# Sixteen-head attention as one stream of quads, with the second pass two quads behind the first

## The chip, the cores and the metric

The program runs on one core of a Trainium2 chip. The metric is the device time in microseconds (us); lower is better. TensorE is called PE, VectorE DVE, ScalarE ACT, GpSimd POOL, and SP is the engine that issues the DMAs.

## The reference

Eight layers are added to a residual stream `x` of 8 sequences of 512 tokens of 128 features in float32. The change is in two of them, both 16-head softmax attention with heads of 8 features:

```python
x = x + _L0_attn_a_ref(_layernorm(x), ...)   # causal: where(tril, q@k.T, -inf) / sqrt(128)
x = x + _L0_ffn_ref(_layernorm(x), ...)
x = x + _L0_attn_b_ref(_layernorm(x), ...)   # not causal, rope on the input, q@k.T / sqrt(8)
x = x + ...                                  # six more layers, untouched
# in both: q,k,v = xn@W.T + b per head; softmax(q@k.T) @ v; all heads @ Wo.T + bo
```

## The kernel before

An *item* is a sequence (8), a *quad* is four heads (4 in an item, 32 in a layer). `attention` is built twice: `aa` (causal) and `ab` (with rope).

- Preparation of an item: layer norm (DVE L450 to L471, POOL L236, L252), transposition to `xT` (PE L345, ACT L315), projections q and k (PE L353, ACT L319) and v (PE L359, DVE L480, POOL L248). q and k are each cut into three bfloat16 parts by four dependent instructions (`split_part`, L214): q on POOL, k on DVE. SP stores the six parts in DRAM (`store`, L279) and loads them back, rearranged, as `QS` and `KS` in two halves of eight heads, 18 DMAs of 64 KB each (`stack`, L286).
- First pass (`first_scores` L362): scores with queries on the partitions, two banks of PSUM; DVE takes the row maxima straight from them (L488). Of a quad that is 16 matmuls of 512 keys in `ab`; in `aa` 128 to 512 keys, and each is followed by a mask matmul (L377). When a quad is done DVE makes its negated maxima in two bfloat16 parts (`nm`, L492, L494), PE transposes them (L384), DVE copies them out (L500), SP stores them in DRAM and, when that has landed, loads them into two rows of `QS` (`send_nm`, L297). They all go through SP's one queue, in which `stack` and `store` stand too.
- Second pass (`scores` L387): scores with keys on the partitions, maxima subtracted by those two rows; it needs `nm_loaded` of its quad. In `aa` a mask matmul follows each (L402). ACT takes the exponentials (L332, four buffers `probs`), and PE multiplies them with V (`sum_keys` L406), one group of 4 heads per key tile, each head in its own 32 columns of the array. DVE copies the sums out (L506), PE turns them (`tail`), DVE divides (L511, L513). After four quads come `oT` and `y` (L434) and the residual (L520).

The order is one list `STEP` that all engines walk, each in order and each waiting on semaphores. Preparation, first pass, second pass and output are four stages, each one whole item behind the other: a quad's second pass comes four quads after its first. Eleven steps run in all, the middle four as a hardware loop.

Of the kernel before, what the change touches and what calls it, by code (L numbers as in the profile page):

```python
# [25 lines left out]
P = 128  # L26
# [56 lines left out]
SHIFT_ROWS = 2  # L83


def score_units(causal):

    if not causal:
        first = [(qt, (j,), 512, 512) for qt in range(4) for j in range(4)]
        second = [(kt, pair, 512, 512) for kt in range(4) for pair in ((0, 1), (2, 3))]  # L90
        return first, second
# [4 lines left out]
    return first, second  # L96


def attention(core, items, w, causal, rope, scale):
    nc, X, ps = core["nc"], core["X"], core["ps"]  # L100
    first, second = score_units(causal)
    N1, N2 = len(first), len(second)
# [32 lines left out]

# [18 lines left out]
    nm_ready, nmT_ready = sem("nm_ready"), sem("nmT_ready")  # L154
    nm_loaded = [sem(f"nm_loaded{i}") for i in range(QUADS)]
    scores_ready, scores_free = sem("scores_ready"), sem("scores_free")
    probs_free, sums_free = sem("probs_free"), sem("sums_free")
    STACK_DMAS = 2 * SPLITS * SPLITS

    PREP, PASS1, PASS2, OUT = range(4)  # L160

    extra = {(0, 0): [("ln1", 0), ("vaug", 0)], (0, N2 // 2): [("ln2", 0)], (1, 0): [("xT", 0)],
             (1, 3): [("q", 0)], (1, 5): [("k", 0)], (2, 0): [("k split", 0)], (2, 1): [("k split", 1)],
             (2, 2): [("k split", 2)], (2, 3): [("k split", 3), ("store", 0), ("half0", 0)],
             (3, 3): [("v", 0)]}

    last_quad = {(0, 1): [("last sums", 3), ("last nm", 3)], (0, 2): [("last tail", 3)],  # L170
                 (0, 3): [("oT", 0)], (0, 5): [("y", 0)]}
    STEP, waiting = [(0, "half1", 1)], []
    for hq in range(QUADS):
        for i in range(N2):
            mine = range((i * N1 + N2 - 1) // N2, ((i + 1) * N1 + N2 - 1) // N2)
            STEP += [(hq, "first", u) for u in mine[:1]]
            STEP += [(hq, "scores", i)]
            STEP += [(hq, "first", u) for u in mine[1:]]
            STEP += waiting
            waiting = []  # L180
            if i == N2 - 1 or second[i + 1][0] != second[i][0]:
                waiting.append((hq, "sum", second[i][0]))
            if hq and i == 1:
                STEP += [(hq, "sums", hq - 1), (hq, "nm", hq - 1)]
            if hq and i == 2:
                STEP += [(hq, "tail", hq - 1)]
            STEP += [(hq, what, j) for what, j in last_quad.get((hq, i), [])]
            STEP += [(hq, what, j) for what, j in extra.get((hq, i), [])]
    STEP += waiting

    stage_of = {"ln1": PREP, "ln2": PREP, "xT": PREP, "q": PREP, "k": PREP, "k split": PREP, "v": PREP,
                "store": PREP, "half0": PREP, "half1": PASS1,
                "vaug": PASS1, "first": PASS1, "nm": PASS1,
                "scores": PASS2, "sum": PASS2, "sums": PASS2, "tail": PASS2,
                "last nm": PASS2, "last sums": OUT, "last tail": OUT, "oT": OUT, "y": OUT}
    USES = ("xT", "q", "k", "v", "nm", "last nm", "tail", "last tail", "oT", "y")

    def walk(eng, does):


        def step(s, par, on):
            m = (4 * done(s, PREP, items) + 3 * done(s, PASS1, items) + 4 * done(s, PASS2, items)
                 + 3 * done(s, OUT, items))
            for hq, what, i in STEP:
                k = stage_of[what]
                if on(k):
                    part = does.get(what.replace("last ", ""))
                    if part is not None:
                        part(s - k, hq, i, (par - k) % 2, m)
                    if what in USES:  # L210
                        m = m + 1
        run_steps(eng, items, 4, step, before=1)

    def split_part(eng, a, n, m, i):  # L214


        src, parts = proj[a], split[a]
        if i == 0:


            eng.wait_ge(misc_free, m + 1)
            wait(eng, stack_loaded[1], 16 * STACK_DMAS * n)
            eng.tensor_tensor(parts[0][:], src[:], core["zeros"][:], ALU.add)
        if i == 1:
# [9 lines left out]
    def gpsimd(g):
# [6 lines left out]
        def vaug(n, hq, i, par, m):  # L241


            if isinstance(n, int) and n == 0:
                g.wait_ge(set_up, 1)
# [1498 lines left out]
```

## Time and profile before

| | |
|---|---|
| median of 3 runs | 2516.82 us (2515.82 to 2524.92) |
| profiled execution, first to last instruction | 2520.3 us |
| PE / DVE / ACT / POOL busy | 1994.8 / 1683.3 / 850.6 / 502.1 us |
| layer `aa`, first score to residual | 61.3 to 568.2 us |
| layer `ab`, first score to residual | 671.0 to 1239.8 us |

The profiled execution's own time is its span, 2520.3 us; nothing outside the span is shown for it. Busy shares are averages over nine layers with different limits, so the two attention layers are read by themselves.

### The profile page before, as it was taken

What the parts mean: (1) busy time and instruction counts of PE and PEld (TensorE: products, weight loads), DVE (VectorE), ACT (ScalarE), POOL (GpSimd) and SP (SyncE); (2) the same over time, 40 slices, a digit from 0 to 9 for tenths busy, and PEclk for the clock granted to TensorE, in tenths of its full rate; (3) what the DMA queues carried; (4) which work ended last, traced back from release to release, by engine and by line L of the source; (5) the groups of instructions that cost most, each with busy time, mean ns of one, the idle gap of its engine ahead of it and who ended that gap; (6) DMA issues with size and microseconds to landing.
All of it is one profiled execution on the core that took longest, in us unless ns stands there. A gap on an engine that the chain in (4) does not pass through costs nothing. (4 is left out here: it accounts for less than half of the span.)

```text
span 2520.3 us, 37035 instructions
## 1 busy us (share of the span) xinstructions
PE 1994.8 (79%) x12009; PEld 1174.1 (47%) x12009; DVE 1683.3 (67%) x3783; ACT 850.6 (34%) x1324; POOL 502.1 (20%) x421
## 2 busy tenths in 40 slices
PE   1688887885388998899669999999999856668566
PEld 0244444443122222222237777777778534445344
DVE  1666666646388877887257776677666469945897
ACT  0033343353025545556542222322232322223122
POOL 1111111003221111110120000000000446620566
PEclk9788888896569989999789999999999978879787
DMA  6333333200323222221000000000000000000000
GB/s 151 61 54 56 53 53 52 52 2 2 50 52 52 52 52 52 43 46 15 1 0 1 1 1 1 1 1 2 1 1 1 1 0 1 0 1 0 5 13 17
DMA packets 71728, 63.01 MB, mean 25 GB/s; under 512 B 11528, under 2 KB 69384, under 8 KB 71560
## 3 DMA queue, kind: packets, MB, share of 16 engines
q1 hardware_dynamic: 71560, 60.87, 13.7%
q8 instruction: 93, 1.52, 0.3%
q14 instruction: 75, 0.61, 0.1%
HBM read 45.51 MB, written 15.20 MB: 24 GB/s over the span
## 5 line engine op out<-in xcount | busy, mean ns | idle before, releaser
L488 DVE TENSOR_REDUCE ab_M<-ps 128x1 f32<-128x512 f32 x512 | 331.3, 686 | 91.8 <-PE ps L372 76.4
L332 ACT ACTIVATE ab_probs<-ps 128x1024 f32<-128x1024 f32 x256 | 260.3, 1024 | 250.9 <-PE ps L399 248.9
L488 DVE TENSOR_REDUCE aa_M<-ps 128x1 f32<-128x384 f32 (+3 forms) x352 | 216.3, 639 | 157.6 <-PE ps L377 144.9
L372 PE MATMUL ps<-ab_KS,ab_QS 72*128 72x512 bf16 x512 | 217.4, 430 | 74.6 <-DVE ab_M L488 40.0
L332 ACT ACTIVATE aa_probs<-ps 128x1024 f32<-128x1024 f32 (+1 forms) x192 | 168.4, 882 | 284.3 <-PE ps L402 282.2
L372 PE MATMUL ps<-aa_KS,aa_QS 72*128 72x384 bf16 (+3 forms) x512 | 156.1, 340 | 121.3 <-DMA aa_KS<-aa_parts_dram 89.5
L1439 PE MATMUL ps<-gate_up,fp_xT 128*128 128x352 f32 x256 | 127.9, 665 | 91.3 <-DVE fp_xh L1481 90.3
L372 PEld LDWEIGHTS ps<-ab_KS,ab_QS 72*128 72x128 bf16 x512 | 51.3, 100 | 263.1 <-DVE ab_M L488 205.3
L416 PE MATMUL ps<-ab_probs,ab_V 128*9 128x512 f32 x1024 | 145.6, 643 | 21.3 <-ACT ab_probs L332 15.9
L399 PE MATMUL ps<-ab_QS,ab_KS 74*128 74x512 bf16 x512 | 160.1, 399 | 0.5 <-ACT ab_probs L332 0.5
L372 PEld LDWEIGHTS ps<-aa_KS,aa_QS 72*128 72x128 bf16 x512 | 54.5, 107 | 192.2 <-DMA aa_KS<-aa_parts_dram 65.3
L1007 PE MATMUL ps<-la_V,la_S 128*128 128x65 f32 x1024 | 142.5, 262 | 0.1
L1007 PEld LDWEIGHTS ps<-la_V,la_S 128*128 128x128 f32 x1024 | 134.6, 191 | 0.5 <-issue 0.5
L1439 PEld LDWEIGHTS ps<-gate_up,fp_xT 128*128 128x128 f32 x256 | 68.0, 278 | 137.8 <-issue 69.6
L399 PE MATMUL ps<-aa_QS,aa_KS 74*128 74x256 bf16 (+3 forms) x512 | 130.7, 320 | 0.8 <-ACT aa_probs L332 0.4
L984 PEld LDWEIGHTS ps<-la_phiq,la_phik 64*128 64x128 f32 x1024 | 108.6, 187 | 45.7 <-issue 22.5
L1071 DVE TENSOR_TENSOR la_S<-ps,keep_kq 128x512 f32<-128x512 f32 x128 | 84.8, 686 | 64.9 <-PE ps L984 64.9
L984 PE MATMUL ps<-la_phiq,la_phik 64*128 64x128 f32 x1024 | 126.2, 285 | 0.0
L937 ACT ACTIVATE la_attnT<-ps 128x512 f32<-128x512 f32 x64 | 38.2, 597 | 256.0 <-PE ps L1015 256.0
L558 POOL TENSOR_TENSOR la_rstd<-la_vare,mhalf 128x4 f32<-128x4 f32 x16 | 16.1, 1008 | 518.0 <-DVE la_vare L553 518.0
L377 PE MATMUL ps<-mask_qk,ident 128*128 128x128 bf16 x512 | 112.8, 244 | 0.0
L416 PE MATMUL ps<-aa_probs,aa_V 128*9 128x512 f32 (+3 forms) x1024 | 98.8, 459 | 6.1 <-DVE aa_C L506 2.4
(286 smaller groups left out, 3981.3 us busy)
## 6 DMA issues: line engine op xcount, KB each, us to landing
aa_QS<-aa_parts_dram SPq DMA_DIRECT2D x144, 64.0 KB
aa_KS<-aa_parts_dram SPq DMA_DIRECT2D x144, 64.0 KB
ab_QS<-ab_parts_dram SPq DMA_DIRECT2D x144, 64.0 KB
ab_KS<-ab_parts_dram SPq DMA_DIRECT2D x144, 64.0 KB
aa_parts_dram<-aa_splitq SPq DMA_DIRECT2D x24, 128.0 KB, 1.8
aa_parts_dram<-aa_splitk SPq DMA_DIRECT2D x24, 128.0 KB, 1.8
ab_parts_dram<-ab_splitq SPq DMA_DIRECT2D x24, 128.0 KB, 1.8
ab_parts_dram<-ab_splitk SPq DMA_DIRECT2D x24, 128.0 KB, 1.8
```

Of the source, the lines that this page charges most:

```text
L332: act.activation(v(probs[r][:]), v(src), ACT.Exp, scale=scale).then_inc(scores_free, 1)
L372: last = pe.matmul(ps[:, FIRST + b, o * stride:o * stride + width], QS[par][0:ROWS, h, qt * P:(qt + 1) * P], KS[par][0:ROWS, h, 0:width], ...
L377: last = pe.matmul(ps[:, FIRST + b, c:c + P], core["ident16"][:], core["mask_qk"][:], start=False, stop=True)
L399: last = pe.matmul(ps[:, bank, c:c + width], KS[par][0:rows, h, kt * P:(kt + 1) * P], QS[par][0:rows, h, 512 - width:512], start=True, sto ...
L416: last = pe.matmul(ps[32 * j:32 * j + DH + 1, SUMS, 512 - width:512], V[par][:, kt, 4 * hq + j, :], probs[(N2 * hq + i) % 4][:, o * stride ...
L488: v.tensor_reduce(M[:, heads[0]:heads[-1] + 1, qt], src, AX.X, ALU.max).then_inc(max_free, 1)
L558: g.tensor_tensor(rstd[par][:], vare[par][:], mhalf[:, 0:per], ALU.pow).then_inc(rstd_ready, 1)
L937: act.activation(flat(attnT[:]), misc, ACT.Copy).then_inc(misc_free, 1)
L984: last = pe.matmul(ps[:, SCORES + a, cols], phi[1][j % 2][rows, cols], phi[0][j % 4][rows, cols], start=True, stop=True)
L1007: last = pe.matmul(dst[:, AUG * a:AUG * (a + 1)], S[a][j % 2][:, c * P:(c + 1) * P], V[par][:, c, 2 * j + a, :], start=c == 0, stop=c == 0 ...
L1071: v.tensor_tensor(S[a][j % 2][:].rearrange("p (c q) -> p c q", c=4), ps[:, SCORES + a, :].rearrange("p (c q) -> p c q", c=4), over(core["k ...
L1439: last = pe.matmul(ps[:, GATE_UP + 2 * t + i, 0:INNER], xT[p][:, t * P:(t + 1) * P], gate_up[:, i, :], start=True, stop=True)
```

## The change

Both layers are rewritten on one list of events, fully unrolled, sorted by a time counted in quads (`attention_order`). Quad g has its first pass at times g to g+1, its second pass at g+2 to g+3. An item n is prepared from t0 = 4(n-1) on; its first pass begins at t0+4. In a steady item the list runs, for PE, POOL and SP in the same order:

```text
t0+1.03 xT   1.17 q   1.20 split q   1.30 nm(quad 0 of item n-1)   1.55 k   1.58 split k
t0+2.30 nm(quad 1)   2.33 store   2.50 load half 0   3.12 v   3.30 nm(quad 2)   3.40 load half 1
t0+4.00 first pass of item n   4.04 scores of quad 2 of item n-1   4.30 nm(quad 3)   5.04 scores of quad 3
```

```diff
+    for n in range(items):
+        t0 = QUADS * (n - 1)
+        ...
+        at(t0 + 1.17, "q", n, 0)
+        at(t0 + 1.20, "split", n, 0, 0)
+        at(t0 + 1.55, "k", n, 0)
+        at(t0 + 1.58, "split", n, 0, 1)
+        at(t0 + 2.33, "store", n, 0)
+        at(t0 + 2.50, "half", n, 0, 0)
+        at(t0 + 3.40, "half", n, 0, 1)
+        for q in range(QUADS):
+            g = QUADS * n + q
+            ...
+            at(g + 1.30, "nm", n, q)
+            for i, t in enumerate(s_at):
+                at(g + LAG + t, "scores", n, q, i)
+            ...
+    # POOL
+        def split_part(n, q, gq, a):
+            if n or a == 0:
+                split_into(g, a, n)          # the four dependent instructions
+        def negate(n, q, gq, i):
+            g.wait_ge(max_free, N1 * (gq + 1))
+            ...
+            g.tensor_scalar(nm[:, 0], M[gq % 2][:], -1.0, None, ALU.mult)
+            g.drain()
+            g.tensor_tensor(nm[:, 1], M[gq % 2][:], nm[:, 0], ALU.add).then_inc(nm_ready, 1)
+        def clear_future(n, q, gq, i):       # causal only, once for each unit of exponentials
+            g.wait_ge(scores_free, u + 1)
+            g.affine_select(out=diagonal, in_=diagonal, ..., fill=0.0, ...).then_inc(probs_masked, 1)
     # PE, first pass and second pass: the mask matmuls go
-                if causal:
-                    last = pe.matmul(ps[:, FIRST + b, c:c + P], core["ident16"][:], core["mask_qk"][:], ...)
-                if causal:
-                    last = pe.matmul(ps[:, bank, c:c + P], core["ident16"][:], core["mask_kq"][:], ...)
     # PE, sums: in pieces of at most 256 queries (8 for a quad of ab, 6 of aa; before 4)
+        pieces = [(kt, lo, lo + 256) for kt in range(4) for lo in (0, 256)]
     # DVE, maxima in the causal layer: one instruction for each head (16 for a quad, before 11)
+                for o, j in enumerate(heads):
+                    last = v.tensor_tensor_reduce(masked[U % 4][:, ...], src[:, o, :], mask_row[:, 512 - width:512],
+                                                  1.0, 4 * NEG, ALU.add, ALU.max,
+                                                  accum_out=M[gq % 2][:, j, qt:qt + 1])
     # to ACT: the copies of v, nm (from L500) and the sums (from L506)
+            act.activation(V[n % 2][:, :, :, 0:DH], misc4..., ACT.Copy)
+            act.activation(nmT[q][:], misc.bitcast(BF16)[0:32, 0:P], ACT.Copy)
+            act.activation(C[:]..., ps[:, SUMS, :], ACT.Copy)
```

The bias of v is folded once into that of the output, the maxima `M` have two buffers, the ranges of `nm` change sign with the constant rows of `KS`, and waits name constants.

## Rows read from the trace of the kernel before

**Rows 1.** Windows by stage: window, length, each engine's busy us (instructions), PE clock, DMA share, GB/s
```profile
61.30:115.70 54.40, 33.15 (x154) 14.89 (x155) 35.46 (x73) 1.97 (x3) 8.37 (x7) 0.73 0.38 57
115.70:528.00 412.30, 344.07 (x2976) 188.47 (x2977) 267.97 (x585) 162.51 (x192) 51.61 (x43) 0.87 0.32 51
528.00:567.50 39.50, 33.85 (x317) 16.74 (x309) 7.61 (x21) 21.92 (x27) 0.00 (x0) 0.96 0.01 1
...
671.00:725.00 54.00, 40.74 (x79) 10.13 (x79) 45.88 (x87) 3.25 (x4) 12.19 (x11) 0.53 0.33 52
725.00:1185.50 460.50, 413.30 (x2096) 131.20 (x2100) 374.19 (x733) 243.20 (x248) 74.85 (x67) 0.92 0.27 46
1185.50:1237.50 52.00, 39.37 (x239) 11.86 (x232) 7.28 (x18) 32.24 (x34) 0.00 (x0) 0.96 0.00 1
```

**Rows 2.** Waits of layer aa: total us, times, longest us
```profile
PE ps L372 <- DMA aa_KS<-aa_parts_dram: 54.0, 6, 11.1
```

**Rows 3.** SP's timeline: start us, us, instruction; a cycle of aa, two halves of ab
```profile
196.58 0.31 SPq L300 DMA_DIRECT2D aa_nm_dram<-aa_nmT  x1
197.93 0.22 SPq L302 DMA_DIRECT2D aa_QS<-aa_nm_dram  x1
...
214.04 1.30 SPq L283 DMA_DIRECT2D aa_parts_dram<-aa_splitq  x3
...
218.22 3.34 SPq L294 DMA_DIRECT2D aa_QS<-aa_parts_dram  x9
...
224.75 0.32 SPq L300 DMA_DIRECT2D aa_nm_dram<-aa_nmT  x1
234.33 0.23 SPq L302 DMA_DIRECT2D aa_QS<-aa_nm_dram  x1
234.81 3.06 SPq L294 DMA_DIRECT2D aa_QS<-aa_parts_dram  x9
...
254.33 0.23 SPq L302 DMA_DIRECT2D aa_QS<-aa_nm_dram  x1
...
713.08 3.08 SPq L294 DMA_DIRECT2D ab_QS<-ab_parts_dram  x9
...
729.30 0.23 SPq L302 DMA_DIRECT2D ab_QS<-ab_nm_dram  x1
...
1128.21 3.07 SPq L294 DMA_DIRECT2D ab_QS<-ab_parts_dram  x9
...
1147.45 0.23 SPq L302 DMA_DIRECT2D ab_QS<-ab_nm_dram  x1
```

**Rows 4.** Groups of instructions: us busy, mean ns of one, idle before
```profile
L488 DVE TENSOR_REDUCE ab_M<-ps 128x1 f32<-128x512 f32 x512 | 331.3, 686 | 91.8 <-PE ps L372 76.4
...
L377 PE MATMUL ps<-mask_qk,ident 128*128 128x128 bf16 x512 | 112.8, 244 | 0.0
...
L416 PE MATMUL ps<-aa_probs,aa_V 128*9 128x512 f32 x256 | 39.3, 690 | 4.3 <-DVE aa_C L506 2.4 <-ACT aa_probs L332 1.4
...
L416 PE MATMUL ps<-aa_probs,aa_V 128*9 128x256 f32 x256 | 19.8, 381 | 0.0
```

**Rows 5.** Timeline of PE and POOL around one projection and split of q
```profile
198.95 1.07 PE L353 MATMUL ps<-aa_xT,w_wq 128*128 128x512 f32 x2
...
200.83 1.28 POOL L223 TENSOR_TENSOR aa_splitq<-aa_q,zeros 128x512 bf16<-128x512 f32 x1 [10.89 <-ACT aa_q L319]
...
204.97 1.16 POOL L229 TENSOR_TENSOR aa_splitq<-aa_restq,aa_splitq 128x512 bf16<-128x512 f32 x1
```

**Rows 6.** Windows after a stall of aa, columns as in rows 1
```profile
350.00:352.50 2.50, 0.00 (x0) 0.00 (x0) 0.00 (x0) 0.00 (x0) 0.00 (x0) 0.50 0.56 99
...
362.50:365.00 2.50, 2.50 (x13) 0.39 (x11) 1.11 (x2) 0.81 (x1) 0.49 (x1) 0.50 0.58 78
```

**Rows 7.** Nearest rows to the new operations: a group, and POOL's start
```profile
L1165 ACT ACTIVATION_READ_ACCUMULATOR qs_E<-ps,qs_nbias 128x1 f32 x32 | 6.7, 208 | 0.0
```
```profile
3.41 0.30 POOL L1611 TENSOR_SCALAR_AFFINE_SELECT keep_kq<-keep_kq 128x128 f32<-128x128 f32 x1
```

More of the change, by code:

```diff
@@ L83 @@
 SHIFT_ROWS = 2
+LAG = 2
 def score_units(causal):
@@ L95, in score_units, with attention_order, at @@
     second += [(2, (0, 1, 2, 3), 256, 256), (3, (0, 1, 2, 3), 128, 128)]
-    return first, second
+    pieces = [(0, 0, 256), (0, 256, 512), (1, 128, 256), (1, 256, 512), (2, 256, 512), (3, 384, 512)]
+    return first, second, pieces
+def attention_order(items, causal):
+    slots = QUADS * items
+    found = []
+    def at(time, what, n, q, i=0):
+        found.append((time, len(found), what, n, q, i))
+    if causal:
+        f_at = [u / 11 for u in range(11)]
+        s_at = [0.04, 0.20, 0.36, 0.50, 0.66, 0.82]
+        sum_at = [0.46, 0.55, 0.77, 0.87, 1.05, 1.19]
+        copy_at = 1.23
+    else:
+        f_at = [u / 16 for u in range(16)]
+        s_at = [(i + 0.25) / 8 for i in range(8)]
+        sum_at = [at / 4 for at in (1.875, 2.11, 2.375, 2.875, 3.375, 3.875, 4.375, 4.63)]
+        copy_at = 1.20
+    at(-4, "bias", 0, 0)
+    for n in range(items):
+        t0 = QUADS * (n - 1)
+        for t in range(4):
+            at(t0 + 0.02 + 0.09 * t, "stat", n, 0, t)
+        at(t0 + 0.39, "spread", n, 0)
+        for t in range(4):
+            at(t0 + 0.53 + 0.06 * t, "norm", n, 0, t)
+        at(t0 + 0.74, "turn", n, 0)
+        at(t0 + 1.03, "xT", n, 0)
+        at(t0 + 1.17, "q", n, 0)
+        at(t0 + 1.20, "split", n, 0, 0)
+        at(t0 + 1.55, "k", n, 0)
+        at(t0 + 1.58, "split", n, 0, 1)
+        at(t0 + 3.12, "v", n, 0)
+        at(t0 + 2.33, "store", n, 0)
[3 more added lines that the diff above has]
+            g = QUADS * n + q
+            for u, t in enumerate(f_at):
+                at(g + t, "first", n, q, u)
+            at(g + 1.30, "nm", n, q)
+            for i, t in enumerate(s_at):
+                at(g + LAG + t, "scores", n, q, i)
+            for i, t in enumerate(sum_at):
+                at(g + LAG + t, "sum", n, q, i)
+            at(g + LAG + copy_at, "copy", n, q)
+            at(g + LAG + 1.44, "tail", n, q)
+        at(QUADS * n + 3 + LAG + 1.62, "oT", n, 0)
+        at(QUADS * n + 3 + LAG + 1.82, "y", n, 0)
+    return [event[2:] for event in sorted(found)]
@@ L99, in attention @@
 def attention(core, items, w, causal, rope, scale):
     nc, X, ps = core["nc"], core["X"], core["ps"]
-    first, second = score_units(causal)
-    N1, N2 = len(first), len(second)
+    first, second, pieces = score_units(causal)
+    N1, N2, N3 = len(first), len(second), len(pieces)
     name = "aa" if causal else "ab"
@@ L134, in attention @@
     oT = sb("oT", [P, 4, P])
+    if causal:
+        mask_row = sb("mask_row", [P, 512])
+        masked = [sb(f"masked{i}", [P, 512], BF16) for i in range(4)]
     parts_dram = nc.dram_tensor(f"{name}_parts_dram", [2, SPLITS, P, 512], BF16, kind="Internal").ap()
@@ L165, in attention @@
[L165 to L212, printed above, removed]
@@ L234, in gpsimd @@
[L234 to L256 removed]
+    order = attention_order(items, causal)
@@ new lines, in attention, with uses_of_misc, walk, last_unit @@
+    USES = ("bias", "xT", "q", "k", "v", "nm", "tail", "oT", "y")
+    turn_of = {use: at for at, use in enumerate(e[:3] for e in order if e[0] in USES)}
+    def uses_of_misc(what, n, q=0):
+        return turn_of[what, n, q] + 1
+    def walk(does):
+        for what, n, q, i in order:
+            if what in does:
+                does[what](n, q, QUADS * n + q, i)
+    def last_unit(kt):
+        return max(i for i in range(N2) if second[i][0] == kt)
+    def last_piece(kt):
+        return max(p for p in range(N3) if pieces[p][0] == kt)
@@ L1650, in attention_weights, with column @@
     return pick
+def column(v):
+    return v.rearrange("(p o) -> p o", o=1)
 def row(v):
```

415 lines of the change are left out of this document (225 added, 190 removed).

## The prediction

> **What bounds the kernel now.** I read the stage windows first [rows 1]. The reader sees that the two attention layers take 506.9 us (`aa`, 61.3 to 568.2) and 568.8 us (`ab`, 671.0 to 1239.8), and that each has three parts: a first pass alone (54.4 and 54.0 us), seven items in which everything overlaps (412.3 and 460.5 us, so 58.9 and 65.8 us for an item), and a second pass alone (39.5 and 52.0 us, and about 7 us of closing steps, part of them past the window). In the middle part of `aa` PE is busy 344 of 412 us and DVE 268; in that of `ab` PE 413 and DVE 374 of 460.5. The waits come second [rows 2]: in `aa` PE stood 54.0 us in 6 waits for `KS`, up to 11.1 us at a time. Third, SP's timeline [rows 3] says why: half a stack is begun at 218.22 and the little `nm` store that SP issues behind it at 224.75 has landed only by 234.33, when the next instruction goes. So half a stack occupies the queue for 16.1 us, the next one (234.81 to 254.33) for 19.5 us. Over the 14 halves of `aa` that follow the fill the mean is 17.9 us (15.7 to 19.8), over those of `ab` (first 713.08, last 1128.21) 16.4 us (13.0 to 19.3). An `nm` exchange on a free queue takes 1.35 us to its second leg (196.58 to 197.93). Before, the delayed `nm` costs nothing, because its scores come four quads after its first pass. `aa` is bound by PE plus this DMA chain, `ab` by PE and DVE handing banks to each other.
>
> **The load of a quad after the change.** Causal layer. PE loses 32 mask matmuls of 128 columns a quad [rows 4]; at 2.4 GHz such a one is worth some 0.058 us of PE (128 columns, estimated), so 1.9 us a quad. Its score matmuls are 4 each of 128, 256, 384 and 512 columns in each pass: 5120 columns, 2.2 us with starts, 4.5 us for both. The sums: 32 groups of 512 queries were busy 39.3 us, 32 of 256 were busy 19.8 [rows 4], so 1.23 and 0.62 us, and two halves cost as much as a whole plus at most a start of some 0.13 us; 6 pieces come to 2.9 us. With `nm`, the turn of the sums and a quarter of an item's preparation (2.0 us together) PE needs 9.4 us. DVE: a 512-wide maximum is 0.686 us [rows 4]; one of 128 takes 0.29 by its 384 fewer elements at 0.96 a ns (estimated). Sixteen of four widths make 7.8 us, where eleven made 6.8, plus what the accumulator costs. No row has that on DVE. Below, it is nothing, or 1 us a quad less than nothing where the next one overlaps; above, the 0.208 us that ACT's accumulator read takes [rows 7], 3.3 us a quad; I take 1.0, nearer to the low end, as a read of one column beside DVE's own stream. With division, norm and residual (1.5 us) DVE needs 10.3 us (8.3 to 12.6). A causal quad then takes a little over the larger sum, 10.8 us (9.8 to 13), where nothing else stops it. In `ab`, PE has 32 matmuls of 512 (7 us), 8 half pieces (4.4), and 2.0 to 2.4 of the rest: 13.4 us; DVE is relieved of copies, `nm`, the v bias and the split of k (2.3 us a quad) and falls to 11.7. I take 14.5 us for a quad (13.4 to 15), against 16.4 now. The copies that go to ACT are hidden: it was busy 162.5 of 412 and 243 of 460 us [rows 1] and stays under 10 us a quad (were it full, they would cost 1 us a quad). POOL in `aa` gains six clears: 0.30 us for 128 columns [rows 7], 256 and 512 here, estimated 0.4 and 0.7 (0.3 to 1.2), 3 us; `nm` as two small instructions, 0.6 us (0.3 to 2.5, the latter if each took the 1.28 us of a 512-column one [rows 5]); and the split of k. As sums these hide; as a queue they do not, below.
>
> The Trainium skill ("VectorE: DVE Perf Modes", Two Vector instructions with no wait between them) says that an op which also writes out its accumulator is two instructions, the main one and an accumulator read. That speaks against the change; no run here shows its price on DVE. If it cost what ACT's does, the sum would be that of the third rival.
>
> **What lies on the path.** Time is counted in quads as in the list. Call V the moment when PE turns `nm` of quad 1 (t0+2.30). SP must send that `nm` first: PE and ACT 1.2 us, exchange 1.35 us, so the store of the parts starts at V+2.6. From a store to its first load are 4.2 us (214.04 to 218.22) [rows 3]. Half 0 then holds the queue for 17.9 us; `nm` of quad 2 (t0+3.30) is behind it, and its second leg lands some 1.7 us after its issue (bounded by 1 and 3; only the first leg's 1.35 is shown). So the scores of quad 2, which stand at t0+4.04, can't start before V+2.6+4.2+17.9+0.3+1.7 = V+26.7. PE is there by itself after 1.74 quads, 18.8 us in `aa`: a stall of 8 us. Half 1 goes behind that exchange, and `nm` of quad 3 behind half 1: its scores (5.04) start at V+26.7+17.9+0.3 = V+44.9, against one quad after 26.7: 7 us more stall. In `ab`, with 16.4 us a half, these two are V+25.2 and V+41.9; there the stalls are 0 and 2.2 us.
>
> Then the next item's q. POOL's queue has the split of q (1.20) ahead of `nm` (1.30), and PE stands at the turn of `nm` with first-pass matmuls, scores and sums of everything queued behind it, so DVE and ACT run dry too. From the q matmul to the end of the split the trace has 198.95 to 206.13, 7.2 us [rows 5]; `nm` adds 0.6: 7.8 us. In `aa` a clear that waits for an exponential stands ahead of the split, 1.5 us: 9.3. Before, `nm` was on DVE and this cover was there. PE's own work between the two is 1.8 us, so the stall is about 6 us in `ab` and 7.5 in `aa`. (If the list let the split run ahead, it would be nothing.) In `aa` the clear behind the split of k (1.66 behind 1.58) makes the sums at 2.05 late by about 2.5 us. The clock goes with the stalls: after some 7 us of idle it is 1.2 GHz, in 350.0 to 352.5, and still in 362.5 to 365.0 with PE wholly busy [rows 6], about 10 us of work at half speed, which cost some 4.3 us of a quad that needs 9.4 PE us of 10.8. For late sums and clock together I take 4.6 us an item in `aa` (0 to 8); in `ab`, where the idle is shorter, 2 (0 to 5).
>
> The period of an item, V to V: `aa` 44.9 + 0.13 quad 1.4 + 9.3 + one quad 10.8 + 4.6 = 71 us; it was 58.9. `ab` 41.9 + 1.9 + 7.8 + 14.5 + 2 = 68; it was 65.8. A shorter quad helps only 1.1 of 4 times, because the DMA chain covers the rest.
>
> **Sum.** `aa`: 30 us to the first V (1.2 quads of first pass alone, the q stall, one quad), 6 periods 426, 44.9 to the scores of the last item's predecessor, 3 quads without preparation 30.5, two quads of second pass alone at 7.6 (8.5 now less 0.9 of masks) and some 6.3 of closing (of the 40 us of before, the rest after four quads): 552.9, against 506.9: +46. `ab`: 37 + 408 + 41.9 + 40 + 2 x 11.8 + 7 = 557.5, against 568.8: -11. The lag of two instead of four quads is what saves some 25 us at each layer's ends, and is in these. The seven other layers stay. So 2520.3 + 35 = 2555 in the profiled execution, whose span is 3.5 above the median of the runs; for the median 2552 us. Its own range: periods of 66 to 75 and 65 to 71 us, 2504 to 2594.
>
> **Rivals.**
> 1. Faster, by the cover at q: the same DMA chain, but PE doesn't stand at 1.30 and the clock stays up. It decides if POOL is through with the split and `nm` within two us of PE's arrival. Then the periods are 60 and 62.5 us: `aa` 485 (-22), `ab` 522 (-46), in all -68: 2449 us. For it: all stalls are between engines that then find work waiting. Against: 7.2 us in rows 5 for 0.13 quad of cover.
> 2. Faster by much: neither `nm` is late. The items then run at 4 quads, 58 us in `ab` and 45 in `aa` (where the queue is full with 4.2 + 2 x 17.9 + some 5 us): `aa` 376, `ab` 491, so about 2310 us. For it: a free exchange takes 3 us of 8 to 11 available. Against: the 9.6 us between 224.75 and 234.33.
> 3. Slower by DVE: the causal maximum with accumulator costs 0.3 us more than I took, or two cycles an element. A quad of 13 to 15.5 us gives 6 x 1.13 x (2.2 to 4.7) more, and 5 quads of it at the ends, 26 to 55 us: 2578 to 2607. For it: no row of such an op. Against: the chain covers three quads of four.
> 4. The saved ends and the stalls cancel (periods 66 and 65): 2510 us, no change.
>
> **Chances.** Forecast 0.48, rivals 0.20, 0.07, 0.12 and 0.13. About 0.5% (12.6 us) is what can be told from no change. Slower: 0.45 of the forecast and rival 3, 0.57. Faster: rivals 1 and 2 and 0.01 of the forecast, 0.28. Same: rival 4 and 0.02 of the forecast, 0.15. The range takes in rival 1 and most of rival 3 and leaves out rival 2: 2445 to 2605 us.
>
> **What would show it.** In the trace after: `nm` stores on SP whose second leg comes 8 to 12 us later, directly behind each half, and PE waiting after them for a DMA into `QS`, twice an item in `aa`; PE's turn of `nm` waiting about 6 us for POOL once an item; periods between the stores of parts of 66 to 75 us (`aa`) and 65 to 71 (`ab`); DVE under two thirds busy in `aa`; the clock at 1.2 GHz in more than a third of `aa`; the second passes alone halved. I am wrong if the periods are under 62 us, or if a DVE maximum is the longest wait in `aa`.

## The result, and the profile after

The changed kernel takes 2671.03 us (median of 4 runs, 2656.02 to 2687.41), the kernel before 2516.32 beside it (4 runs, 2509.56 to 2524.92): a ratio of 1.062, 95% interval 1.056 to 1.067. It is slower, as forecast, but by 155 us instead of 35, and outside the range. The changed kernel timed once more in a later group of runs took 2634.47 us, 1.051 (1.042 to 1.060). The interval of one group does not hold what the kernel does in another; differences below some 1% between kernels of different groups are not read below. Runs more than 1.5% above the fastest of the same kernel are in the medians, but not in the ratios.

The stages of the profiled execution (2685.7 us). Columns as in [rows 1]: window, length, busy us of PE, PEld, DVE, ACT, POOL, PE's clock as a share of 2.4 GHz, DMA share, GB/s.

```profile
57.30:89.70 32.40, 19.56 (x55) 6.63 (x55) 19.25 (x95) 4.29 (x6) 13.64 (x16) 1.00 0.24 34
89.70:544.70 455.00, 340.69 (x2193) 131.66 (x2193) 204.79 (x897) 163.38 (x221) 151.03 (x252) 0.69 0.25 43
588.30:664.00 75.70, 63.11 (x432) 23.60 (x432) 25.86 (x106) 31.65 (x42) 16.27 (x38) 0.68 0.01 2
...
760.70:799.30 38.60, 26.55 (x52) 6.57 (x52) 25.28 (x50) 5.57 (x7) 16.68 (x18) 0.54 0.16 27
799.30:1262.50 463.20, 413.28 (x2578) 129.70 (x2577) 282.16 (x513) 230.04 (x269) 106.17 (x132) 0.81 0.25 43
1313.20:1402.00 88.80, 84.12 (x516) 24.40 (x514) 36.90 (x62) 45.51 (x52) 1.55 (x7) 0.73 0.01 2
...
57.30:664.10 606.80, 462.31 (x2928) 177.31 (x2928) 271.75 (x1187) 216.13 (x292) 189.73 (x326) 0.70 0.23 40
760.70:1402.00 641.30, 572.64 (x3440) 175.49 (x3440) 375.89 (x675) 306.43 (x357) 125.67 (x162) 0.78 0.22 38
```

The windows are cut as the sum was: to the first V, six periods, the 44 or 51 us that follow (left out), the end. Layer `aa` takes 606.8 us (forecast 552.9, before 506.9), `ab` 641.3 (forecast 557.5, before 568.8); the rest of the program is 7 us shorter. The clock column is what differs most: 0.70 and 0.78, where the same two layers had 0.86 and 0.88 before. PE is busy for 462 us in `aa`, against 411, with 32 mask matmuls a quad fewer, and for 573 us in `ab`, against 495. Of the 100 us that `aa` is longer, 51 are busy time; `ab` has 78 us more of it and 5 us less idle.

PE's waits in these layers (us in total, times, longest); the stall at q (L463) is in the first two rows, and in the first of them is also the wait of 1.9 us that every quad of `aa` has:

```profile
PE ps L463 <- POOL aa_nm L296: 97.6, 32, 7.2
PE ps L463 <- POOL ab_nm L296: 40.1, 7, 5.9
PE ps L455 <- DMA aa_KS<-aa_parts_dram: 44.2, 4, 34.1
PE ps L455 <- DMA ab_KS<-ab_parts_dram: 23.6, 4, 20.8
PE ps L478 <- DMA aa_QS<-aa_nm_dram: 10.6, 7, 3.5
```

The new operations by shape (busy us, mean ns, idle before and its releaser):

```profile
L573 DVE CUSTOM_DVE_ANT_0 aa_masked<-ps,aa_mask_row 128x512 bf16<-128x512 f32 x128 | 87.1, 691 | 66.6 <-PE ps L455 66.1
L304 POOL TENSOR_SCALAR_AFFINE_SELECT aa_probs<-aa_probs 128x256 f32<-128x256 f32 x128 | 52.5, 410 | 297.8 <-ACT aa_probs L392 297.8
L573 DVE DVE_READ_ACCUMULATOR2_ANT aa_M<- 128x1 f32 x512 | 42.6, 83 | 0.0
L304 POOL TENSOR_SCALAR_AFFINE_SELECT aa_probs<-aa_probs 128x512 f32<-128x512 f32 x64 | 40.4, 637 | 69.7 <-ACT aa_probs L392 69.5
L573 DVE CUSTOM_DVE_ANT_0 aa_masked<-ps,aa_mask_row 128x128 bf16<-128x128 f32 x128 | 29.4, 286 | 41.8 <-PE ps L455 41.8
L463 PE MATMUL ps<-ident,aa_nm 128*32 128x128 bf16 x32 | 8.8, 275 | 97.6 <-POOL aa_nm L296 97.6
L380 ACT ACTIVATE aa_nmT<-ps 32x128 bf16<-32x128 bf16 x32 | 8.5, 267 | 67.4 <-PE ps L463 67.4
L294 POOL TENSOR_SCALAR aa_nm<-aa_M 128x16 bf16<-128x16 f32 x32 | 8.2, 256 | 0.0
```

POOL's queue, in start order, around one of the seven stalls at q, and then PE's. Clear, four instructions of the split, then `nm`; PE's last matmul before it ends at 369.5:

```profile
370.50 0.41 POOL L304 TENSOR_SCALAR_AFFINE_SELECT aa_probs<-aa_probs 128x256 f32<-128x256 f32 x1 [3.50 <-ACT aa_probs L392]
370.87 1.26 POOL L249 TENSOR_TENSOR aa_splitq<-aa_q,zeros 128x512 bf16<-128x512 f32 x1
...
374.97 1.15 POOL L255 TENSOR_TENSOR aa_splitq<-aa_restq,aa_splitq 128x512 bf16<-128x512 f32 x1
376.09 0.26 POOL L294 TENSOR_SCALAR aa_nm<-aa_M 128x16 bf16<-128x16 f32 x1
```
```profile
369.20 0.33 PE L455 MATMUL ps<-aa_KS,aa_QS 72*128 72x384 bf16 x1
376.77 0.29 PE L463 MATMUL ps<-ident,aa_nm 128*32 128x128 bf16 x1 [7.24 <-POOL aa_nm L296]
```

And a quad with no preparation beside it. Here too `nm` is behind a clear, which waits for an exponential (611.22), and PE stands 1.86 us:

```profile
611.22 0.41 POOL L304 TENSOR_SCALAR_AFFINE_SELECT aa_probs<-aa_probs 128x256 f32<-128x256 f32 x1 [3.04 <-ACT aa_probs L392]
611.60 0.25 POOL L294 TENSOR_SCALAR aa_nm<-aa_M 128x16 bf16<-128x16 f32 x1
612.00 0.22 POOL L296 TENSOR_TENSOR aa_nm<-aa_M,aa_nm 128x16 bf16<-128x16 f32 x1
```
```profile
612.27 0.29 PE L463 MATMUL ps<-ident,aa_nm 128*32 128x128 bf16 x1 [1.86 <-POOL aa_nm L296]
```

SP's timeline of one item of `aa`, answering to [rows 3]. V is 544.7. The halves begin at V+6.6 and V+24.1, and the store of `nm` issued at 559.99 is followed by its second leg only at 568.51:

```profile
546.94 1.45 SPq L324 DMA_DIRECT2D aa_parts_dram<-aa_splitq  x3
...
551.27 3.08 SPq L336 DMA_DIRECT2D aa_QS<-aa_parts_dram  x9
...
559.99 0.32 SPq L342 DMA_DIRECT2D aa_nm_dram<-aa_nmT  x1
568.51 0.23 SPq L344 DMA_DIRECT2D aa_QS<-aa_nm_dram  x1
568.79 3.07 SPq L336 DMA_DIRECT2D aa_QS<-aa_parts_dram  x9
...
577.30 0.32 SPq L342 DMA_DIRECT2D aa_nm_dram<-aa_nmT  x1
586.78 0.23 SPq L344 DMA_DIRECT2D aa_QS<-aa_nm_dram  x1
```

Last, the clock. One whole quad of `aa`, from `nm` to `nm`, at the end of the layer, where no preparation is left; below it a quad with the same matmuls from the second profile of the same kernel (e15), at the high clock. Then a window of 65 us at the end of `ab`, and the 5 us behind it:

```profile
595.00:612.50 17.50, 15.64 (x87) 5.16 (x87) 7.83 (x34) 6.05 (x8) 3.35 (x8) 0.50 0.01 2
```
```profile
401.50:412.50 11.00, 8.86 (x85) 3.51 (x85) 8.37 (x38) 6.05 (x8) 3.33 (x8) 1.00 0.45 83
```
```profile
1361.00:1366.00 5.00, 5.00 (x39) 1.37 (x37) 3.67 (x7) 3.79 (x5) 0.47 (x2) 1.00 0.00 2
1295.00:1360.00 65.00, 65.00 (x281) 17.26 (x279) 31.52 (x50) 23.87 (x28) 0.94 (x4) 0.50 0.09 12
```

At 1.2 GHz (0.50) a quad of `aa` takes 17.5 us and PE is busy in 89% of it; at 2.4 GHz (1.00) it takes 11.0 us, with PE busy in 81%. In `ab` PE is busy in all of 65 us by the records, and the clock stays at 0.50; then it is 1.00, with PE as busy. The stretches of low clock here are 559 to 624 and 1289 to 1361 us.

### The profile page after: what moved, and what is told of

Its sections match the earlier page's. It is cut to its first block and busy times, and to the rows that moved or that the text cites. A ratio compares the mean times of both kernels' runs of the same rounds, so it can differ in the third digit from the quotient of the medians.

```text
span 2685.7 us, 37409 instructions
## 1 busy us (share of the span) xinstructions
PE 2135.7 (80%) x12525; PEld 1158.5 (43%) x12525; DVE 1588.5 (59%) x4129; ACT 911.6 (34%) x1470; POOL 672.1 (25%) x784
## 5 line engine op out<-in xcount | busy, mean ns | idle before, releaser
L578 DVE TENSOR_REDUCE ab_M<-ps 128x1 f32<-128x512 f32 x512 | 341.7, 689 | 252.3 <-PE ps L455 250.5
L573 DVE CUSTOM_DVE_ANT_0 aa_masked<-ps,aa_mask_row 128x384 bf16<-128x384 f32 (+3 forms) x512 | 233.4, 488 | 329.5 <-PE ps L455 328.6
L392 ACT ACTIVATE ab_probs<-ps 128x1024 f32<-128x1024 f32 x256 | 262.1, 1024 | 240.6 <-PE ps L478 239.4
L455 PE MATMUL ps<-ab_KS,ab_QS 72*128 72x512 bf16 x512 | 229.0, 466 | 32.6 <-DMA ab_KS<-ab_parts_dram 23.6
L455 PE MATMUL ps<-aa_KS,aa_QS 72*128 72x384 bf16 (+3 forms) x512 | 167.2, 401 | 49.5 <-DMA aa_KS<-aa_parts_dram 44.2
L478 PE MATMUL ps<-ab_QS,ab_KS 74*128 74x512 bf16 x512 | 185.9, 450 | 6.5 <-DMA ab_QS<-ab_nm_dram 6.4
L498 PE MATMUL ps<-ab_probs,ab_V 128*9 128x256 f32 x2048 | 189.0, 448 | 0.6 <-ACT ab_probs L392 0.6
L304 POOL TENSOR_SCALAR_AFFINE_SELECT aa_probs<-aa_probs 128x256 f32<-128x256 f32 (+1 forms) x192 | 92.6, 486 | 367.6 <-ACT aa_probs L392 367.4
L498 PE MATMUL ps<-aa_probs,aa_V 128*9 128x256 f32 (+1 forms) x1536 | 144.5, 462 | 16.4 <-POOL aa_probs L304 16.4
L478 PE MATMUL ps<-aa_QS,aa_KS 74*128 74x256 bf16 (+3 forms) x512 | 142.5, 395 | 10.6 <-DMA aa_QS<-aa_nm_dram 10.6
```

The source lines that it names most:

```text
L304: g.affine_select(out=diagonal, in_=diagonal, compare_op=ALU.is_ge, fill=0.0, base=0, pattern=[[0, len(heads)], [1, P]], channel_multiplie ...
L392: act.activation(v(probs[u % 4][:]), v(src), ACT.Exp, scale=scale).then_inc(scores_free, 1)
L455: last = pe.matmul(ps[:, FIRST + U % 2, o * stride:o * stride + width], QS[n % 2][0:ROWS, h, qt * P:(qt + 1) * P], KS[n % 2][0:ROWS, h, 0: ...
L478: last = pe.matmul(ps[:, bank, c:c + width], KS[n % 2][0:rows, h, kt * P:(kt + 1) * P], QS[n % 2][0:rows, h, 512 - width:512], start=True, ...
L498: last = pe.matmul(ps[32 * j:32 * j + DH + 1, SUMS, lo:hi], V[n % 2][:, kt, 4 * q + j, :], probs[(N2 * gq + u) % 4][:, c:c + hi - lo], sta ...
L573: last = v.tensor_tensor_reduce(masked[U % 4][:, o * stride:o * stride + width], src[:, o, :], mask_row[:, 512 - width:512], 1.0, 4 * NEG, ...
```

## The experiments

All are timed beside the kernel before. `aa` and `ab` are the lengths of the layers in the profiled execution, in us, with the clock; that of e8, one of its two slowest executions, is not used. A profiled execution can lie off the median: that of the changed kernel is the slowest of its four (2687 us), those of e1, e5 and e12 are the fastest of theirs (2535, 2497 and 2565 us), so layer lengths differ by more than the kernels do.

| kernel | us | ratio (95%) | `aa`, clock | `ab`, clock |
|---|---|---|---|---|
| before | 2516 | 1 | 507, 0.86 | 569, 0.88 |
| changed | 2671 | 1.062 (1.056-1.067) | 607, 0.70 | 641, 0.78 |
| changed, again | 2634 | 1.051 (1.042-1.060) | 593, 0.71 | 597, 0.86 |
| e1 split of q behind `nm` | 2550 | 1.017 (1.008-1.026) | 553, 0.72 | 538, 0.89 |
| e2 second pass three quads behind | 2602 | 1.035 (1.028-1.043) | 583, 0.69 | 586, 0.88 |
| e3 mask matmuls in addition | 2634 | 1.051 (1.041-1.062) | 589, 0.81 | 597, 0.86 |
| e4 filler matmuls before waits | 2716 | 1.080 (1.069-1.091) | 646, 0.73 | 600, 0.93 |
| e5 `nm` on VectorE | 2523 | 0.999 (0.995-1.003) | 514, 0.76 | 546, 0.89 |
| e8 e1 + `nm` ahead of the clear | 2524 | 1.001 (0.997-1.004) | - | - |
| e6 e1 + exchange on ScalarE's queue | 2594 | 1.033 (1.025-1.042) | 592, 0.72 | 565, 0.88 |
| e12 masks as before | 2596 | 1.034 (1.025-1.044) | 545, 0.85 | 582, 0.87 |
| e7 e1 + masks as before | 2492 | 0.984 (0.977-0.991) | 499, 0.89 | 554, 0.87 |
| e13 e1 without clears | 2482 | 0.988 (0.980-0.996) | 488, 0.86 | 551, 0.88 |
| e10 e7 + stack in quarters | 2515 | 0.996 (0.992-0.999) | 507, 0.86 | 572, 0.84 |
| e9 e7 + three quads behind | 2445 | 0.973 (0.966-0.979) | 450, 0.94 | 538, 0.91 |
| e11 e7 + whole sums | 2469 | 0.980 (0.974-0.986) | 493, 0.88 | 536, 0.93 |
| e14 e9 + whole sums | 2429 | 0.966 (0.960-0.973) | 462, 0.92 | 530, 0.94 |
| e16 e8 + three quads + whole sums | 2435 | 0.968 (0.963-0.974) | 480, 0.82 | 528, 0.95 |

My theory (A in the first expectations) was that PE's waits for GpSimd cost what they last plus a clock that recovers within 10 us; the rival (B) that the clock, once down, stays down and carries most of the loss.

**e1, the split of q behind `nm`.**

```diff
-        at(t0 + 1.20, "split", n, 0, 0)
+        at(t0 + 1.31, "split", n, 0, 0)
```

> Changed kernel with one event moved: POOL's split of q stands at t0+1.31, behind nm (1.30), instead of at 1.20. Theory A (stalls as priced in the prediction, the clock a small addition): PE's wait of 6 to 7 us for nm of quad 0 goes in 14 items, 80 us plus a little clock: about 2585 us. Theory B (the 1.2 GHz clock is the main loss and any stall sets it off; PE has 2 to 3 of them an item): this stall goes but the other two keep the clock down, 40 to 130 us gained, 2540 to 2630. Theory C (the order on POOL does not matter, DVE or PE bound by their own work): 2660 to 2680.

One number in the list brings back 121 us beside the first measurement of the changed kernel, 84 beside the second. The result lies 35 us under the value of theory A and in the range of B; C is refuted. In `ab` POOL's wait is gone and the layer is 31 us shorter than before the change. In `aa` the 7.2-us waits are gone, and what is left is the clear's:

```profile
PE ps L463 <- POOL aa_nm L296: 60.2, 31, 2.2
```

The stall at q was six waits of 7.2 us and one of 6.0 in `aa`, and 40 us in 7 times in `ab`. Of these 89 us 78 are gone, because behind it the clear's 1.9 us come to light. So the stall cost what it lasts, or up to half as much again.

**e2, the second pass three quads behind the first.**

```diff
-LAG = 2
+LAG = 3
-        at(t0 + 3.12, "v", n, 0)
+        at(t0 + 4.12, "v", n, 0)
```

> Changed kernel with a lag of three quads instead of two (LAG = 3; v one quad later, at t0+4.12, because its buffer is free a quad later). nm then has 1.74 quads of cover instead of 0.74. Theory A: the waits of the second pass for nm behind a half stack go (aa 22.9 us and ab 14.3 us of idle PE by the trace, and the clock behind them), the wait for half 0 stays, the ends cost one quad more (about 15 us a layer): net 0 to -40, 2630 to 2670 us. Theory B: the clock recovers too, -60 to -120: 2550 to 2610. If the SP chain is the bound of an item as I predicted, the period of aa falls from 75.6 us to under 65.

2602 us: in the range of B, though only 32 us under the second measurement of the changed kernel. PE's 17 us of waits for `nm` to land are gone, the POOL waits are as before (97.0 us in 32 times in `aa`), and the clock in `aa` is no higher, so B's reason isn't borne out there. The period of `aa` fell from 75.8 to 70.3 us, not under 65: in the changed kernel the DMA chain alone does not set the period.

**e3, the mask matmuls issued in addition.** The mask is applied twice.

```diff
+                if causal:
+                    last = pe.matmul(ps[:, FIRST + U % 2, c:c + P], core["ident16"][:], core["mask_qk"][:],
+                                     start=False, stop=True)
```

(and the same in the second pass.)

> Changed kernel with the 1024 mask matmuls of the causal layer issued again (the masks of VectorE and GpSimd stay), so PE has 1.9 us more work a quad at full clock, 3.7 us at half. Theory A (the masks were PE work and are rightly gone): slower by 30 to 110 us, 2700 to 2780. Theory B2 (those full-width bfloat16 matmuls are what let the clock come back in the layer before the change; after it the clock stays at 1.2 GHz for 65 us on end with PE 90% busy): the share of 1.2 GHz in aa falls and the kernel is no slower, or faster by up to 60 us, 2610 to 2670.

1024 more matmuls in `aa` cost nothing: 2634 us, as the second measurement of the changed kernel. The clock in `aa` is 0.81 instead of 0.71, PE's busy time 460 us instead of 457: B2 of the expectation, and A is refuted. In these two profiled executions the higher clock made up for the added work.

**e4, filler matmuls before the waits.** 20 matmuls without use ahead of `nm` of quad 0, 14 ahead of the second pass of quads 2 and 3.

```diff
+            if q == 0 and n < items - 1:
+                for _ in range(20):
+                    pe.matmul(misc, QS[n % 2][0:ROWS, 4 * q, 0:P], KS[n % 2][0:ROWS, 4 * q, 0:512],
+                              start=True, stop=True)
```

> Changed kernel with idle PE time filled: 20 matmuls of 512 columns before PE waits for nm of quad 0 and 14 before it waits for the nm load of quads 2 and 3, into banks that the next real matmul overwrites; 4.3 and 3.0 us of PE at 2.4 GHz, twice that at 1.2. Theory A: nothing waits less, the fill is hidden where the stall is longer and costs where it is shorter: 0 to +80 us, 2670 to 2750. Theory B (the clock is the main loss): PE stays near 2.4 GHz in both layers, its mean clock rises from 0.82 to over 0.87, and the kernel gains 40 to 120 us, 2550 to 2630.

The stall is filled (the longest POOL wait is 2.9 us) and `ab` is granted 0.93, but the kernel is slower, 2716 us beside 2671 and 2634, as theory A of its expectation said: fillers also run where the wait is short, and at 1.2 GHz they last twice as long. PE was busy 550 of 646 us in `aa`. As a cure it failed; as a test of A against B it says only that a high clock is no gain if PE pays for it.

**e5, `nm` on VectorE again**, at 1.15 quads; **e8, e1 and `nm` on GpSimd at 1.17**, ahead of the second clear (1.20).

```diff
+            at(g + 1.15, "neg", n, q)
 ...
-        does = {"spread": root, "turn": turn, "split": split_part, "nm": negate}
+        does = {"spread": root, "turn": turn, "split": split_part}
 ...
+              "neg": negate, "first": maxima,
```

> One part of the change undone: the negated maxima are made on VectorE again (at 1.15 quads), all else as in the changed kernel. Theory A (PE's turn of nm waits in GpSimd's queue, for the split of q once an item and in the causal layer for a clear that waits for an exponential in each quad): both go, so it must be faster than moving the split alone (2550 us, ratio 1.017): the 31 waits of 60 us in all that were left there in the causal layer go too, 2480 to 2530 us. Rival B (what was left beside the split is the DMA chain and the clock, and the wait for nm is cover that something else takes): 2535 to 2565 us. Rival C (VectorE becomes late by the two small instructions): above 2570 us.

> The split of q stands behind nm, and GpSimd makes nm at 1.17 quads, ahead of the second clear (1.20), instead of at 1.30 behind it. Beside 2550 us with the split moved alone. Theory A (the clear in front of nm costs 60 us in the causal layer, and some clock with it): 2480 to 2520 us, the same as nm on VectorE. Rival B (cover, something else is late next, for instance the maxima themselves): 2535 to 2560 us.

2523 and 2524 us: the same, and 26 us under e1 by the medians (44 and 40 by the ratios, since the kernel before ran 11 us faster beside e1), where 60 us of waits went. e5 came out at the upper end of theory A, e8 4 us above its range. It is the place in the queue that costs, not the engine.

**e6, the exchange on ScalarE's queue.**

```diff
+            act.dma_start(nm_dram[q], nmT[q][:]).then_inc(nm_stored, 16)
 ...
+            act.wait_ge(nm_stored, 16 * (gq + 1))
+            act.dma_start(QS[n % 2][ROWS:ROWS + SHIFT_ROWS, 4 * q:4 * q + 4],
```

> The split of q stands behind nm, and both legs of the nm exchange are issued by ScalarE (second leg 0.3 quad behind the first) instead of standing in SP's queue behind the halves of the stack. Beside 2550 us with the split moved alone. Theory A (the DMA chain of SP is a term of its own, as I predicted: 28 us of PE waits in 15 times for nm to land, and more hidden in the store of the parts): 2500 to 2530 us, and PE's waits for the nm load fall under 5 us in all. Rival B (the chain no longer binds, because quads are slower than I took): 2540 to 2560 us. Rival C (the data of a half delays the exchange on any queue, and ScalarE then stands too): above 2560 us.

44 us slower than e1: rival C. PE's waits for `nm` to land are 52 us in both layers, where e1 had 13. ACT's timeline shows why, in one of the late cases (start, us, engine):

```profile
234.97 0.31 ACTq L383 DMA_DIRECT2D aa_nm_dram<-aa_nmT  x1
...
245.18 0.23 ACTq L387 DMA_DIRECT2D aa_QS<-aa_nm_dram  x1
245.46 0.60 ACT L411 ACTIVATE aa_oT<-ps 128x512 f32<-128x512 f32 x1 [6.00 <-DMA aa_nm_dram<-aa_nmT]
```

On another engine's queue the small store still lands 10.2 us after its issue, with a half's data in flight (the median of all is 1.4), and now ScalarE's own work waits behind it. The Trainium skill ("DMA: Bandwidth & Descriptors", Issuing engines are not separate DMA queues) says that DMAs of all issuing engines end on the same 16 DMA engines and interleave; these rows agree.

**e7 and e12, the causal masks as before**: mask matmuls in both passes, VectorE's plain maximum, no clears; e7 with the split moved, e12 without.

```diff
-                    last = v.tensor_tensor_reduce(masked[U % 4][...], src[:, o, :], mask_row[:, 512 - width:512], ...
+                v.tensor_reduce(M[gq % 2][:, heads[0]:heads[-1] + 1, qt], src, AX.X, ALU.max).then_inc(max_free, 1)
 ...
-        if causal:
-            does["scores"] = clear_future
```

> The split of q stands behind nm, and the causal masks are mask matmuls and VectorE's plain maximum again, without clears on GpSimd. Beside 2550 us with the split moved alone. Theory A (the clears cost more on the path than the mask matmuls did: nm stands behind a clear that waits for an exponential, about 1.9 us of PE a quad, 60 us in all, against some 1.9 us of PE work a quad that now comes back, with the clock higher): 2500 to 2540 us. Rival B (the masks on VectorE and GpSimd are a gain of PE time): 2560 to 2600 us.

> The changed kernel (2671 us, ratio 1.062) with the causal masks as before, nothing else: the split of q stays ahead of nm. Theory A (the masks' part of the loss is its own, as it was 58 us on top of the moved split): 2605 to 2625 us. Rival B (the loss of the masks comes only after the split is moved; before that the stall at q hides it): 2640 to 2670 us. Rival C (both feed the clock, and either alone brings most of it back): 2560 to 2600 us.

More work for PE, and e7 takes 58 us less than e1 (82 by the ratios), 8 less than its theory A allowed; e12, alone, 38 to 75 us less than the changed kernel, in the range of its rival C. The clock in `aa` is 0.89 in e7, where e1 has 0.72, and 0.85 in e12, where the changed kernel has 0.70 and 0.71. The two parts of the loss add up within what can be told: 0.045 for the split and 0.027 for the masks make 1.062 to 0.990, measured 0.984.

**e13, which half of the masks.** e1 with the masked maximum kept on VectorE, the mask matmuls of the second pass back, and no clears.

```diff
-        if causal:
-            does["scores"] = clear_future
+                if causal:
+                    last = pe.matmul(ps[:, bank, c:c + P], core["ident16"][:], core["mask_kq"][:],
+                                     start=False, stop=True)
```

> Split of q behind nm; the first pass keeps the change's masked maximum on VectorE, the second pass has mask matmuls again and GpSimd no clears. Beside 2550 us with the clears and 2492 us with both masks as before. Theory A (all that the masks cost is in the clears: 27 us as the queue in front of nm, the rest as sums that wait for a clear): 2485 to 2505 us. Rival B (some 30 us are VectorE's maximum with accumulator and PE's waits for banks of the first pass): 2515 to 2535 us.

2482 us, as e7: the loss of the masks is in the clears. (e13 also puts 512 mask matmuls back on PE; that these alone gain nothing is e3.) VectorE's maximum with its accumulator costs nothing that can be told here.

**e9 to e11 on the base of e7**: three quads behind; the stack in four groups of 9 DMAs, with `nm` between them; the sums in 4 pieces (their events move with them, to 0.55, 0.87, 1.05 and 1.19 in `aa`).

```diff
-        at(t0 + 3.40, "half", n, 0, 1)
+        at(t0 + 3.32, "half", n, 1, 0)
+        at(t0 + 4.32, "half", n, 0, 1)
+        at(t0 + 4.33, "half", n, 1, 1)
 ...
-        pieces = [(kt, lo, lo + 256) for kt in range(4) for lo in (0, 256)]
+        pieces = [(kt, 0, 512) for kt in range(4)]
```

> Split of q behind nm and masks as before (that kernel: 2492 us, ratio 0.984, PE still waits 34 us in 17 times for nm to land), and the second pass three quads behind the first instead of two. Theory A (SP's chain now sets the period; a third quad covers it): the nm waits go, periods 60.4 us in the causal layer fall to 55 to 57, less 4 x 7, plus some 12 us at each layer's ends: 2470 to 2490 us. Rival B (the waits for nm are cover for something else, and the longer ends are paid): 2500 to 2525 us.

> Split of q behind nm and masks as before (2492 us), and the stack issued in four groups of 9 DMAs, one ahead of nm of quad 2, one behind it, two behind nm of quad 3, so that no nm stands behind more than 9 DMAs of data that were issued before it is ready. Theory A (nm of quads 2 and 3 behind 18 DMAs is what binds now): PE's waits for nm fall from 34 us to under 12, 2460 to 2480 us. Rival B (the parts land later now and PE waits for QS and KS instead): 2495 to 2530 us.

> Split of q behind nm and masks as before (2492 us), and the sums in 4 pieces of a key tile again instead of 6 and 8. My prediction priced the halves at a start of 0.13 us each at most: 10 us of PE work in both layers, half of it hidden: 2480 to 2492 us. Rival (the weight loads of half pieces limit PE, whose loads waited 151 us for issue at this line): 2455 to 2478 us. Rival (the halves let PE work earlier and their loss costs more): above 2500 us.

e9: 2445 us, a larger gain than theory A said. The chain is what the third quad covers: the waits for `nm` are gone and an item of `aa` takes 50 to 56 us. e10: rival B, PE waits 74 us for `KS` in `aa` instead of 45, and the `nm` waits (29 us in 13 times) are nearly gone without gain. e11: 2469 us, in the range of the rival by weight loads. But the ratios beside e7 (0.980 and 0.984) are only 0.4% apart and their intervals overlap, so whether the half pieces cost 22 us or the 10 of my price isn't shown, nor is the reason.

**e14 and e16, both gains together, with either masks.** e14 is e9 with whole sums; e16 keeps the change's masks, with e8's order.

> Split of q behind nm, masks as before, second pass three quads behind the first, and the sums in 4 pieces: the two gains so far, 2445 and 2469 us beside 2492, together. If they add: 2420 to 2430 us. If the whole sums gave their 22 us through the chain that a third quad covers anyway: 2438 to 2448 us.

> The change's masks (VectorE maximum, clears on GpSimd) with nm ahead of the clear, the split of q behind nm, the second pass three quads behind and whole sums: differs from the kernel with masks as before, three quads and whole sums (I expect 2420 to 2445 us) in the masks alone. Theory A (the masks cost by what stood behind them, and with cover nothing): within 10 us of that kernel, or faster by PE's saved 1.9 us a quad. Rival B (they cost by themselves, by less PE work in a row and so a lower clock, and by sums behind clears): 25 to 50 us more than that kernel.

2429 and 2435 us ("if they add", and theory A), no difference that can be told, and both beat the kernel before (by 3.4 and 3.2%) and the changed one. In the profiled executions `aa` is 18 us longer with the clears and at 0.82 instead of 0.92. With a third quad of cover and `nm` ahead of the clear, nothing is left of their 58 us in the medians.

**e15, the changed kernel again.**

> The changed kernel once more, for a second profiled execution. Its layer ab took 641 us where three kernels with that layer's code unchanged took 583 (masks undone alone) to 600 us. Theory A (ab has several stable rhythms with the same code, and an execution falls in one or another by what came before): median 2655 to 2690 us again, ab of this profile anywhere in 580 to 645 us. Rival B (the state of the clock that the causal layer leaves makes ab slow in every execution): ab 630 to 650 us again.

The median, 2634 us, is under both ranges; `ab` is in that of theory A, and B is refuted. `ab` took 597 us where it took 641 with the same code. PE was busy for 519 us of it at a clock of 0.86, and for 573 at 0.78, with the same 3440 instructions, and was idle for 78 and 69 us; its waits for POOL were 38 and 40 us. So the 44 us between the two are slower work, not stalls: here the clock by itself made a layer 7% longer. Items of `ab` settle in rhythms: those of the first profile take 67.7 to 82.7 us, those of the second 64.2 to 78.2, and the difference is how often quads fall into the low clock. Why this execution fell so often stays open.

## Why the prediction was wrong

**Right in its times, not in its stalls: the DMA chain.** The scores of quad 2 were put at V+26.7 and those of quad 3 at V+44.9. In `aa` they start at V+26.6 and V+44.1, means over the seven items (25.1 to 28.7, 42.1 to 46.8). Where PE is late, as in `ab`, they slip to V+28.1 and V+48.3, beside 25.2 and 41.9. But PE was to stand 8 and 7 us there in each item of `aa`, and it waited for `nm` to land 10.6 us in 7 times in all eight items, at most 3.5 us. It came to these places late by itself, at the low clock. So it is in part luck that the times agree in `aa`: slow work stands where stalls were forecast, and it hid most of the clock's cost in the sum.

**Right: the stall at q.** Put at 7.5 us in `aa` and about 6 in `ab`; PE waited 7.2 us in six items of `aa`, and 5.7 on the mean of 7 in `ab`. Its mechanism is shown by e1.

**Right: the small prices.** Clears 0.41 and 0.64 us (0.4 and 0.7), `nm` on POOL two instructions of 0.26 and 0.22, the accumulator read 83 ns, 16 of them 1.3 us a quad (1.0), a 128-wide maximum 0.29. Rival 3 is refuted by e13. A quad of `aa` at the high clock takes 11.0 us (10.8), 2 of them the wait for `nm`, one of `ab` 13.3 without preparation and 15.7 with v and the output of an item (14.5).

**Wrong: the clock.** The step was "still in 362.5 to 365.0 with PE wholly busy [rows 6], about 10 us of work at half speed", turned into 4.6 us an item in `aa` and 2 in `ab`. I took the length of one recovery in the kernel before for the length of each. In the changed kernel the low clock lasts up to 65 us at a time in `aa` and 72 in `ab`, over whole quads in which PE is 89 and 100% busy, and such a quad takes 17.5 us instead of 11 in `aa`, 22 to 24 instead of 13 to 16 in `ab`. In the six periods of `aa` the clock was 0.69: 0.62 of the time at 1.2 GHz, 47 us an item, against 15 in the kernel before (0.87 over its seven items). PE was busy 57 us an item in `aa`, where the sum has 4 times 9.4 and 4.6 for clock and late sums. That is 15 us more, and only 5 of them came out in the period, because the DMA chain was to hold PE there anyway. In `ab` it was busy 69 us, where the sum has 4 times 13.4 and 2: 13 more, of which 9 came out. A longer stretch is in the kernel before as well: its first in `aa` lasts 37 us, with PE busy in 59% of it and one wait of 11 us for `KS` inside.

```profile
87.00:124.00 37.00, 21.69 (x98) 9.85 (x98) 19.97 (x46) 2.86 (x3) 2.25 (x2) 0.50 0.44 72
```

It hurts most where the DMA chain gives no cover: the end of `aa` was put at 52 us and took 75.7, the end of `ab` 70.6 and 88.8, 42 of the 130 us by which the sum of the profiled execution was too small. The periods were put at 71 and 68 us and took 75.8 and 77.2; times six that is 84 more; the rest is what `ab` lost behind the last V, 9 us, and small pieces of both signs.

**Wrong: `nm` behind the clear.** "In `aa` a clear that waits for an exponential stands ahead of the split" was priced once an item. The same clear stands ahead of `nm` in all four quads (list: 1.20 and 1.30), 1.9 us of PE each, 60.2 us in 31 times in e1. In the sum it is nothing. e5 and e8 say it was worth 26 us (40 to 44 by the ratios), e13 that the clears in all were worth 68 (72). The other 30 to 40 were not separated: PE's waits for clears in the sums are 16.4 us, 20.1 in e1.

**The rivals.** Of the faster ones, rival 1 is what e8 and e1 make by hand: `ab` falls to 538, but `aa` stays above its 485 with the clears in place. Rival 2 needed periods of 45 and 58 us, and even e9 has 50 to 56 and 57 to 69. Rival 3 fell with e13, rival 4 with the result.

**Not settled.** What keeps the clock down while PE is wholly busy. In `aa` it was 0.85 and more where the clears went (e7, e9, e12, e13), 0.76 where they no longer stood ahead of `nm` (e5), and 0.72 where only the stall at q went (e1); e3 lifted it to 0.81 by work alone. In `ab` e1 and e5 have 0.89, little above the 0.86 to 0.88 of e2, e3, e12 and e15, which keep the stall at q. But e7, e9, e12 and e13 also put mask matmuls back on PE, which e3 shows to lift the clock with the clears in place. So these runs show what the stall at q and the clears cost in time, and not which of them sets off the low clock. No edit moved the clock by itself at no cost to PE. The two executions of the changed kernel do it in `ab`, with nearly the same waits, and differ by 44 us; that the clock carries most of the missing 130 us is read from the windows of the layers.

## What to carry to other kernels

When an operation moves to another engine's in-order queue, price everything ahead of it in that queue in every round, not only the large piece once an item; here the position of one split and one clear was worth more than all instructions saved. A clock loss is to be priced as a state that can last, by the busy time of a whole round at either level, and first where nothing covers PE. When a shorter lag saves the ends of a loop, check it against the transfer it used to hide: one more quad of lag gave 47 us by the medians (29 by the ratios) in e9.

## What the runs showed of the hardware

- TensorE stayed at 1.2 GHz for 65 us in which PE was busy without a gap by the records (1295 to 1360; matmul ends are modelled). The Trainium skill ("TensorE: Matmul & The Clock Gate", What's actually happening) says that activity releases the throttle; in this window a busy PE did not, and what ended it at 1361 is not to be seen in the rows. 1024 added matmuls raised the granted share in `aa` from 0.71 to 0.81 with PE's busy time unchanged (e3).
- VectorE's accumulator read is 83 ns, against 208 ns for ScalarE's [rows 7]. The masked maximum in front of it, which reads a second operand, takes 0.691 us for 512 columns, as the plain one of [rows 4] (0.686).
- A small store landed 10.2 us after its issue beside 64-KB transfers that another engine had issued (e6), against 1.4 us in the median.
- With the same instructions and nearly the same waits, `ab` took 641 us at a mean clock of 0.78 and 597 at 0.86, in two executions of one kernel (the result and e15).
